# One load of six consecutive blocks for each tile of EdgeConv, with the block of a pair chosen by a register

## The reference

```
h   = relu(concat(x[dst], x[src] - x[dst]) @ W1 + b1)         # layer 0, EdgeConv
out = segment_max(h @ W2 + b2, dst)
x   = layernorm(x + out)
sums = segment_sum(edge_attr, src); cnt = segment_sum(1, src) # layer 1
v_e  = sums / max(cnt, 1)
x    = layernorm(x + relu(relu(concat(x, v_e, u) @ W1 + b1) @ W2 + b2))
```

## Time and profile before

| | |
|---|---|
| median of three runs | 17326.13 us |
| profiled execution, its own time | 17326.67 us |
| span of that execution | 17324.9 us |
| POOL busy, share of the span | 12811.2 us, 74% |
| DVE busy | 7639.6 us, 44% |
| PE busy | 4859.9 us, 28% |
| POOL, phase b: first gather to last | 4325.9 to 8459.4 us |

### The profile page before, as it was taken

How to read it: one execution, slowest core, us unless ns; L and a number is a source line. 1 busy time by engine, 2 the same in 40 slices (tenths; PEclk the granted TensorE clock), 3 DMA queues, 4 the chain that set the end, 5 groups by cost and what they waited for, 6 DMA issues and landing times.

```text
span 17324.9 us, 127844 instructions
## 1 busy us (share of the span) xinstructions
PE 4859.9 (28%) x21002; PEld 3804.9 (22%) x21002; DVE 7639.6 (44%) x17556; ACT 1055.0 (6%) x4649; POOL 12811.2 (74%) x13050
## 2 busy tenths in 40 slices
PE   3222222221777777777710000000061000000002
PEld 2111111110666666666500000000040000000001
DVE  6554454543555555555521111111134555555555
ACT  0000000000000000000100000000031000000000
POOL 4777777777777777777667777777766777777775
PEclk7555555555555555555555555555585555555555
DMA  2322222221343333333212222222233333333332
GB/s 79 86 79 75 79 76 76 79 75 57 106 107 106 105 104 105 104 105 104 67 46 53 51 53 53 52 52 51 53 130 116 106 108 106 106 106 106 108 104 56
DMA packets 1464874, 1467.52 MB, mean 85 GB/s; under 512 B 727276, under 2 KB 1226435, under 8 KB 1464678
## 3 DMA queue, kind: packets, MB, share of 16 engines
q1 hardware_dynamic: 1029846, 830.49, 15.9%
q0 software_dynamic: 416960, 533.81, 13.1%
q10 hardware_dynamic: 18000, 102.41, 1.5%
HBM read 863.07 MB, written 602.69 MB: 85 GB/s over the span
## 4 chain that ended last, share of the span: by engine, by line
POOL 40%; issue 17%; PE 11%; DMA 4%; DVE 2%; POOLq 0%; ACT 0%; DVEq 0%; SPq 0%; ACTq 0%
POOL gat L621 39%; PE pair L988 4%; DMA gat<-tab_b,gi 4%; PE bank L977 2%; PE bank L965 1%; PE bank L979 1%; PE pair L1080 1%; DVE ub L1416 1%; POOL start_rows L592 1%; PE pair L1114 0%; PE bank L967 0%; PE bank L1030 0%; PE bank L1031 0%; PE pair L1025 0%; DVE yb L1692 0%
## 5 line engine op out<-in xcount | busy, mean ns | idle before, releaser
L580 POOL DMA_INDIRECT perm<-at,ag_idx x3125 | 3080.4, 986 | 1103.5 <-issue 952.5
L621 POOL DMA_INDIRECT gat<-tab_b,gi x3125 | 3182.3, 1018 | 952.5 <-issue 914.7
L621 POOL DMA_INDIRECT gat<-tab_x,gi x3125 | 2979.5, 953 | 1062.5 <-issue 1062.5
L621 POOL DMA_INDIRECT gat<-tab_t,gi x3125 | 3030.6, 970 | 952.4 <-issue 952.4
L1009 PE MATMUL pair<-ident,tails 128*64 128x128 f32 (+1 forms) x20 | 4.9, 421 | 7953.9 <-DVE tails L1441 4005.0
L988 PE MATMUL pair<-blk,ohb 128*128 128x65 f32 x7500 | 1763.1, 422 | 0.0
L1550 DVE TENSOR_TENSOR run_sb<-p,gat 128x320 f32<-128x320 f32 x625 | 319.1, 511 | 3274.2 <-DMA gat<-tab_x,gi 3274.2
L1009 PEld LDWEIGHTS pair<-ident,tails 128*64 128x64 f32 (+1 forms) x20 | 3.1, 168 | 7955.6 <-DVE tails L1441 4005.8
L988 PEld LDWEIGHTS pair<-blk,ohb 128*128 128x128 f32 x7500 | 1645.3, 329 | 73.6 <-DVE ohb L1380 0.4
L1258 DVE TENSOR_TENSOR oh_s<-iota_bf,st_sh 128x490 bf16<-128x490 bf16 x625 | 418.0, 669 | 1709.3 <-DMA perm<-at,ag_idx 1706.9
L1650 DVE TENSOR_TENSOR pr<-gat,cur 128x320 f32<-128x320 f32 x625 | 306.9, 491 | 1525.7 <-DMA gat<-tab_t,gi 1525.7
(11 more groups left out here) (285 smaller groups left out, 10814.1 us busy)
## 6 DMA issues: line engine op xcount, KB each, us to landing
edge<-start_rows SPq DMA_DIRECT2D x250, 800.0 KB
run<-run_sb SPq DMA_DIRECT2D x250, 800.0 KB, 4.1
blk<-perm SPq DMA_DIRECT2D x750, 165.0 KB, 2.3
run<-run_sb SPq DMA_DIRECT2D x125, 900.0 KB, 4.8
at<-in_edge_attr SPq DMA_DIRECT2D x625, 160.0 KB, 4.7
start_rows<-zeros ACTq DMA_DIRECT2D x125, 800.0 KB, 4.3
tab_t<-trow SPq DMA_DIRECT2D x98, 512.0 KB, 2.6
perm<-at,ag_idx POOLq DMA_INDIRECT x3125
```

The source lines that it names most:

```text
L580: pool.indirect_dma_start(perm_d, rows(perm_d, ag_idx[tp][:, k, s:s + 1]), at[tp][:, s, k, :], None).then_inc(a_sc[tp], 16)
L621: pool.indirect_dma_start(gat[:, k, s, 0:width], None, table, rows(table, gi[tp][:, s, k:k + 1])).then_inc(g_in[k], 16)
```

## The change

SP starts one DMA for six consecutive blocks of each tile, from the block of the tile's first pair (clamped so that six fit), instead of six. There are two buffers of six blocks instead of six of one: when all sums of tile t - 1 are done, its buffer is filled for tile t + 1. A third row of `pair_i` holds the slot of a pair's block among the six, and DVE (in `open_bucket`) and PE (in `bucket_sums`) each read it into a register before they address the block. Four small DVE instructions make that row.

```
-        pair_i = sb("pair_i", [1, 2, NPAIR], I32)
+        pair_i = sb("pair_i", [1, 3, NPAIR], I32)
-        blk = [sb(f"blk{i}", [P, SUB, KEY], F32, EDG) for i in range(PER)]
+        blk = [sb(f"blk{i}", [P, PER, SUB, KEY], F32, EDG) for i in range(2)]
...
-            def load_block(j, i):
-                at_block = sp.value_load(pair_i[0:1, 0, bass.ds(j, 1)], min_val=0, max_val=CL - 1)
-                sp.dma_start(blk[i][:].unsqueeze(1), blocks_d[:, bass.ds(at_block, 1)]).then_inc(p_ld[i], 16)
+            def load_blocks(t, tp):
+                at_block = sp.value_load(pair_i[0:1, 0, bass.ds(t * PER, 1)], min_val=0, max_val=CL - PER)
+                sp.dma_start(blk[tp][:], blocks_d[:, bass.ds(at_block, PER)]).then_inc(p_ld[tp], 16)
...
                     if c == "b":
-                        for i in range(PER):
-                            sp.wait_ge(p_mm, t * PER + (i - PER + 1))
-                            load_block(t * PER + i, i)
+                        sp.wait_ge(p_mm, t * PER)
+                        load_blocks(t + 1, 1 - tp)
...
-            def bucket_sums(j, i, early):
-
+            def bucket_sums(t, tp, i, early):
+
+                j = t * PER + i
+                slot = pe.value_load(pair_i[0:1, 2, bass.ds(j, 1)], min_val=0, max_val=PER - 1)
                 pe.wait_ge(p_oh, j + 1)
...
-                    last = pe.matmul(pair[i % 2][:, 0:AGW], ohb[i % 2][:, s, :], blk[i][:, s, 0:AGW],
+                    last = pe.matmul(pair[i % 2][:, 0:AGW], ohb[i % 2][:, s, :],
+                                     blk[tp][:, bass.ds(slot, 1), s, 0:AGW].rearrange("p a f -> p (a f)"),
...
+            firsts = past[0:1, :].rearrange("a (t i) -> a t i", i=PER)[:, :, 0]
+            link(TS(past[0:1, :], past[0:1, :], float(CL - 1), None, ALU.min))
+            link(TS(pair_i[0:1, 0, :], past[0:1, :], float(CL - PER), None, ALU.min))
+            link(TS(jj_f[0:1, :], firsts, float(CL - PER), None, ALU.min))
+            link(TT(pair_i[0:1, 2, :].rearrange("a (t i) -> a t i", i=PER), past[0:1, :].rearrange("a (t i) -> a t i", i=PER),
+                    spread(jj_f[0:1, :], PER), ALU.subtract))
...
                 j = t * PER + i
-                v.wait_ge(p_ld[i], t * 16 + 16)
+                slot = v.value_load(pair_i[0:1, 2, bass.ds(j, 1)], min_val=0, max_val=PER - 1)
+                if i == 0:
+                    v.wait_ge(p_ld[tp], t * 8 + (16 if tp == 0 else 8))
                 if not (first and i < 2):
                     v.wait_ge(p_mm, j - 1)
                 v.scalar_tensor_tensor(ohb[i % 2][:], spread_mid(iota_bf[:], SUB), lo_of[:, bass.ds(j, 1)],
-                                       spread(blk[i][:, :, AGW], P), ALU.add, ALU.is_equal).then_inc(p_oh, 1)
+                                       spread(blk[tp][:, bass.ds(slot, 1), :, AGW].rearrange("p a s -> p (a s)"), P), ALU.add, ALU.is_equal).then_inc(p_oh, 1)
```

More of the change, by code:

```diff
@@ L188, in gnn_program @@
         endT = sb("endT", [NT, 1], F32, A)
+        jj_f = sb("jj_f", [1, T], F32, A)
         C = ctx_p
@@ L292, in gnn_program @@
         a_sc = [sem(f"a_scat{i}") for i in range(2)]
-        p_ld = [sem(f"p_block{i}") for i in range(PER)]
+        p_ld = [sem(f"p_blocks{i}") for i in range(2)]
         p_oh, p_mm, p_ac, p_zero = [sem("p_" + n) for n in ("onehot", "sums", "added", "zeroed")]
@@ L480, in edge_io @@
                 if c == "b":
-                    for i in range(PER):
-                        load_block(i, i)
+                    load_blocks(0, 0)
+                    load_blocks(1, 1)
                 with loop(sp, 1, T - 3, 2) as t:
@@ L486, in edge_io @@
                 body(T - 2, 1)
[L487 to L490, removed]
                 sp.wait_ge(run_done, (T - 1) * KS)
@@ L999, in phase_b @@
                     for i in SPREAD[k]:
-                        bucket_sums(t * PER + i, i, first and i < 2)
+                        bucket_sums(t, tp, i, first and i < 2)
             each_iteration(pe, phase_b)
@@ L1324, in _ @@
             link(TT(past[0:1, :], jj[0:1, :], pair[0][0:1, 0:NPAIR], ALU.subtract))
-            link(TS(pair_i[0:1, 0, :], past[0:1, :], float(CL - 1), None, ALU.min))
+            firsts = past[0:1, :].rearrange("a (t i) -> a t i", i=PER)[:, :, 0]
[4 more added lines that the diff above has]
+                    spread(jj_f[0:1, :], PER), ALU.subtract))
             TS(pair_i[0:1, 1, :], pair[0][0:1, 0:NPAIR], float(NT - 1), None, ALU.min).then_inc(a_tab, 1)
@@ L1372, in _, with open_bucket @@
             v.wait_ge(p_zero, 1)
-            def open_bucket(t, i, first):
+            def open_bucket(t, tp, i, first):
                 j = t * PER + i
-                v.wait_ge(p_ld[i], t * 16 + 16)
+                slot = v.value_load(pair_i[0:1, 2, bass.ds(j, 1)], min_val=0, max_val=PER - 1)
+                if i == 0:
+                    v.wait_ge(p_ld[tp], t * 8 + (16 if tp == 0 else 8))
                 if not (first and i < 2):
@@ L1417, in phase_b @@
                     for i in SPREAD[k]:
-                        open_bucket(t, i, first)
+                        open_bucket(t, tp, i, first)
                         if i:
```

## The result

| | before | after |
|---|---|---|
| median of 5 runs each, same chip | 17326.13 us (17319.14 to 17334.74) | 17411.08 us (17404.5 to 17414.26) |
| profiled execution | 17326.67 us | 17404.5 us |

The ratio is 1.0047 [1.0036, 1.0059]: the change costs 85 us in the medians and 77.8 us between the profiled executions. The forecast was 17420, in a range of 17325 to 17560.

What follows compares the result with a forecast made beforehand. GpSimd's own gather rate was taken to bound EdgeConv, DVE overlaps stretching gathers. All terms were 0 except DVE's shifted work, 125 tiles x 0.75 = 94 us: 17326.7 + 94 = 17420 us, range 17325 to 17560.

Steps and rivals of the forecast that it cites:

- What bounds the phase: EdgeConv: POOL never waits; its rate, one gather each 1.323 us, is the phase, so only gather duration matters.
- The terms put at zero: One load for six, the larger load, PE's register read and DVE's four table instructions: each taken to cost 0.
- The later landing: Second step of a tile: its gather lands 0 to 2.3 us later behind the 990 KB load; POOL doesn't wait for it.
- the guard: POOL's wait for a third step's bucket sums, 4.9 us of slack; rival of a stall there: 17480 us, 5%.
- PE's read: Register read on PE before its wait for the weights: 0 to 1.9 us in a tile's longest step, taken as 0.
- The shift: DVE's register read makes L1380 begin about 0.95 us after `ub` instead of 0.41; later instructions move by 0.7 us.
- the rival that the prediction built on this sentence: DVE's tensor_tensor doesn't collide with GpSimd's gathers, so time stays 17327 us; 2 in 100, counted within no change.
- The grid term: Shifted DVE instructions cover more gather starts on POOL's grid and stretch those gathers: +0.75 us a tile, 94 us.
- faster: Rival: shifted DVE work misses more gather starts, such as the third step's second L1380 (0.61 us a tile): 17250 us, 8%.
- The tile that I laid out: One tile's gather stretches from the timeline: 2.50 us before, 3.16 after, +0.66 us a tile or 83 us.
- the estimate without a fixed phase: Check with DVE instructions placed at random against gathers: 2.0 us of stretch a tile, 253 us, 22 above today's 231.
- No change: Rival: collisions redistribute to the same sum, or the sequencer reads ahead so L1380 hardly moves: 17327 to 17360 us, 17%.

Runs made afterwards that it cites:

- e1: Kernel before plus one unused register read on DVE ahead of each L1380, six block loads kept: 17461.95 us against 17319.38, ratio 1.0084.
- e4: Changed kernel with DVE's slot reads moved ahead of its wait for the gathered rows, nothing left out: 17291.9 us, ratio 0.9985 to the kernel before.
- e5: Kernel before with one operand of each two-SBUF-operand DVE instruction of EdgeConv moved to PSUM: 17082.04 us against 17316.52, ratio 0.9864.
- e3: Changed kernel without the slot reads on DVE and PE, the one large load kept, some sums wrong: 17315.99 us, ratio 0.9999 to the kernel before.
- e2: Kernel before plus one unused register read on PE ahead of each bucket's products: 17315.92 us, ratio 0.9999.
- e9: Kernel before with operands of DVE and ScalarE instructions moved to PSUM in all four edge phases: 16895.67 us, ratio 0.9756.
- e12: Kernel before plus one unused DVE register read ahead of each L1380, on a chip where the kernel before takes 19927.73 us: 19965.1 us, ratio 1.0014.

## Why the prediction was right

*What bounds the phase* was right: POOL's gaps stayed at 0.30 us, and the phase from its first gather to its last changed by what the gathers' durations changed by, within 0.5 us: +76.9 us in the change, +141.6 in e1, -30.6 in e4 and -233.6 in e5. The whole execution followed less closely, since the other phases vary by some us.

*The terms put at zero* were zero. Fewer loads and the larger load: e3. The later landing came (5.58 us of waiting against 4.49; the mean over the tiles 5.8 against 4.6, within the 0 to 2.3 us) and the guard held: the two buckets of a third step end at 6007.10 (6002.57 + 4.53 in the timeline) and the gather that needs them starts at 6011.36, 4.3 us of slack instead of 4.9. PE's read: e2. DVE's table instructions: phase a's line is the same within 1.3 us, and EdgeConv's first gather starts at 4327.5 instead of 4325.9.

*The shift* was right for the first comparison of a step: 0.97 us from `ub` (0.95 predicted), 0.31 us for the load itself. For the third step's second comparison it was wrong. The prediction moved it "by about as much again", some 1.1 us in all; it moved by 1.55 (1.47 to 3.01 us behind `ub`), more than one turn of the grid of 1.25. In e1, with the read alone, it moved by 1.34, and in e3, with the large load alone, by 0.78, so the large load has a part in where it comes to stand.

*The two sentences of the Trainium skill* (SBUF — State Buffer, "Who interferes with whom"). The first says that in a probe tensor_tensor did not stall DMAs issued by GpSimd. It doesn't carry over to these gathers: in e5, taking one of the two SBUF operands away from five DVE lines, four of them tensor_tensor, shortens them by 234 us. The same place counts tensor_tensor with two SBUF inputs among what contends with GpSimd's reads, so the rival that the prediction built on this sentence rested on one half of the page.

The second is the exclusion, by which whoever is first blocks the other. The prediction wrote "The rows agree", and that holds in one direction only. A gather that starts under such an instruction is longer. But a gather under way doesn't block DVE: 1473 additions and products of before that began over 0.06 us into one took 0.485 us on average and at most 0.494, as those do that began between two gathers. DVE is longer only where the two begin together (0.53 us). What the page gives as free of contention, a DVE instruction with at most one SBUF input, is so here (e5).

*The grid term* was right in its sum, 0.62 us a tile measured against 0.75 taken (+77 against +94 us), and less so in its parts. The comparison's six places in a tile, mean stretch in us, from the same bookkeeping:

```
place in the tile             0     1     2     3     4     5    sum
before                      0.02  0.33  0     0.30  0     0     0.65
after                       0.51  0.20  0.10  0.13  0.04  0.25  1.23
laid out for after          0.56  0     0.09  0.68  0     0.10  1.43
e1                          0.50  0.04  0.24  0.63  0.33  0.24  1.98
```

Place 3 is the second one of the third step. I had it at 0.68 and "0.61 today at each tile"; it costs 0.30 on average before, since it is hit in half of the tiles, and 0.13 after. So the rival *faster* had its mechanism: that instruction did come to start 0.03 us behind a gather. It gave back 0.17 us a tile, not 0.61, and the places 0, 2, 4 and 5 took 0.88. That the sum came out so near is in part luck: place 3 was 0.55 too high, places 1 and 5 were 0.20 and 0.15 too low, and the same grid theory missed e1 (60 us expected, 142.6 measured).

Two further lessons lie in these numbers. The tile that I laid out was not a typical one: its stretch before was 2.4 to 2.5 us, with a mean of 1.86 and nine in ten between 1.1 and 2.5. Taken as a level, my 3.16 for after misses the measured 2.47 by as much as 2.50 misses 1.86. Only the difference of the two, +0.66, was usable, and by itself it would have given 17409 us, closer than what I took after a correction upwards. And the estimate without a fixed phase, 253 us, is far from after (309) and from e1 (374): the phases don't average out, which fits that each `ub` is tied to the gather that it waited for. *No change*, which rested on such an average, had less for it than 17 in 100.

Left open: why the read alone costs 142 us and the read with the large load 78. The table puts the difference into places 2 to 4, behind the step whose gather lands later; that this landing moves them to better phases is argued, not shown.

## What to carry to other kernels

Where GpSimd's indirect DMAs bound a phase, look at the mean against the median of their duration before anything else: here the difference was 0.074 us x 3125 in one phase, and 421 us could be had over four (e9). Put one operand of each DVE instruction that can run beside them into PSUM; until that is done, an edit that shifts DVE by half a microsecond can cost up to 0.8% (e1) or give 0.15% (e4), and says nothing about its own worth. A register read belongs ahead of the engine's long wait, not behind it, even on an engine with much slack.

## What the runs showed of the hardware

- An indirect gather of 128 rows on GpSimd takes 0.944 us plus a gap of 0.305 in EdgeConv, and becomes longer by the remaining time of a DVE instruction with two SBUF operands, less 0.127 us, if that one began more than about 0.05 us before it. With scalar_tensor_tensor as with tensor_tensor; with one operand in PSUM, not at all (0.1 us in total over the gathers that started under L1366, L1389 or L1390). Begun less than 0.02 us before the gather, or 0.03 us after it, the instruction costs the gather nothing.
- The reverse is small: of DVE's additions, those that begin within 0.02 us ahead of a gather take 0.53 us instead of 0.485, and those that begin further inside one take what they always do.
- A register read takes 0.31 us on DVE and 0.30 us on PE. Placed behind a wait on DVE it moved what follows by 0.57 to 0.60 us, and by 0.32 us in the step whose `ub` waits for nothing; ahead of the wait (e4), or on PE (e2), it left the first comparison of each step where it was, at 0.41 to 0.45 us.
- The same kernel takes 17320 us on some chips and 19930 us on two others, at the same granted clock in the profiled executions (0.516 to 0.523). On the latter POOL stands still before many gathers (before 250 of EdgeConv's 3125 in e12, most of them for 1.3 to 3.2 us); the profile puts these waits down partly to "remote", partly to nothing or to an instruction. What causes them is open.
